# Sharing the normalisation between two engines, and gathering before the stage ends, in a graph attention kernel

## The reference

```python
h = relu(layernorm(x))                       # 12500 x 128
hW = (h @ W_node.T).reshape(N, 4, 32)
e  = (edge_attr @ W_edge.T).reshape(E, 4, 32)
att = sum(concat([hW[src], hW[dst], e]) * a) # per head
att = where(att > 0, att, 0.2 * att)
m = maximum(segment_max(att, dst), 0)
ex = exp(att - m[dst])
denom = segment_sum(ex, dst) + (E - deg) * exp(-m)
out = x + segment_sum(ex / denom[dst] * hW[src], dst)
```

## Time and profile before

| | |
|---|---|
| timed runs, median | 2291.24 us |
| profiled execution, its own time | 2286.65 us |
| its span | 2284.8 us |
| stage 1 / stage 2 / stage 3 | 117.1 / 2129.6 / 38.1 us |
| busy share PE, DVE, ACT, POOL | 53, 70, 26, 73% |
| DMA | 199.98 MB, 87 GB/s |

### The profile page before, as it was taken

The page is one execution under the profiler, slowest core; times in us unless marked ns, Lnnn a source line. Parts: engine busy times, 40 slices in busy tenths (PEclk is TensorE's granted clock), DMA queues, the critical chain, the costliest instruction groups (busy, mean ns, idle before and its releaser), DMA issues. The chain is left out here.

```text
span 2284.8 us, 29035 instructions
## 1 busy us (share of the span) xinstructions
PE 1208.8 (53%) x8459; PEld 1009.0 (44%) x8461; DVE 1597.1 (70%) x4440; ACT 602.1 (26%) x1139; POOL 1676.3 (73%) x1778
## 2 busy tenths in 40 slices
PE   4655555555555555555555554555554554544441
PEld 3514444444444444444444443444444444444441
DVE  7317776767777677776777677676767776777677
ACT  3412222222222222222222222222222222222220
POOL 7877777777777777777777777777777777777740
PEclk8976776777776767776766677777767676666665
DMA  3463233323323233232333333232232322223223
GB/s 120 137 215 98 75 93 80 94 75 86 86 74 98 75 98 75 74 99 74 95 78 84 84 78 94 74 98 74 74 99 75 80 56 56 54 55 86 55 81 145
DMA packets 87796, 199.98 MB, mean 88 GB/s; under 512 B 30142, under 2 KB 49502, under 8 KB 81240
## 3 DMA queue, kind: packets, MB, share of 16 engines
q0 software_dynamic: 53120, 112.30, 21.2%
q1 hardware_dynamic: 32631, 79.28, 10.4%
q10 hardware_dynamic: 1888, 6.56, 0.7%
HBM read 181.70 MB, written 16.31 MB: 87 GB/s over the span
## 5 line engine op out<-in xcount | busy, mean ns | idle before, releaser
L698 POOL DMA_INDIRECT gath<-node_table,src_i x1660 | 1580.5, 952 | 511.5 <-issue 492.4
L778 PE MATMUL bank<-vals,onehot 128*128 128x137 f32 x3328 | 693.1, 386 | 595.2 <-DVE vals L1043 364.9
L778 PEld LDWEIGHTS bank<-vals,onehot 128*128 128x128 f32 x3328 | 643.1, 283 | 620.1 <-DVE vals L1043 375.5
L1077 DVE TENSOR_TENSOR acc<-acc,bank 128x137 f32 x1664 | 495.7, 298 | 426.4 <-PE bank L778 157.3
L853 ACT COPY onehot_t<-ps_oht 128x2048 bf16<-128x2048 bf16 x104 | 194.1, 1866 | 1008.4 <-PE ps_oht L748 984.2
L748 PE MATMUL ps_oht<-ident_b,onehot_b 128*128 128x128 bf16 x1664 | 177.7, 292 | 328.1 <-DVE onehot_b L929 328.1
L862 ACT CAST onehot<-onehot_b 128x384 f32<-128x384 bf16 x624 | 268.7, 474 | 254.3 <-PE bank L778 246.8
L748 PEld LDWEIGHTS ps_oht<-ident_b,onehot_b 128*128 128x128 bf16 x1664 | 161.3, 138 | 336.6 <-DVE onehot_b L929 332.4
L1039 DVE TENSOR_TENSOR vals<-gath,bank 128x2048 f32<-128x2048 f32 x104 | 237.2, 2281 | 1.9 <-ACT bank L866 1.7
L929 DVE TENSOR_TENSOR onehot_b<-bank,rel_s 128x2048 bf16<-128x2048 f32 x104 | 237.1, 2282 | 0.0
L730 PE MATMUL bank<-eattr,w_eatt 128*32 128x512 f32 x392 | 184.5, 615 | 8.0 <-DMA eattr<-edge_attr_in 6.6
(11 more groups left out here) (176 smaller groups left out, 964.9 us busy)
## 6 DMA issues: line engine op xcount, KB each, us to landing
eattr<-edge_attr_in SPq DMA_DIRECT2D x49, 1024.0 KB, 5.7
gath<-node_table,src_i POOLq DMA_INDIRECT x1660
node_table<-onehot_b SPq DMA_DIRECT2D x14, 462.0 KB, 4.0
gath<-x_in SPq DMA_DIRECT2D x14, 448.0 KB, 4.9
gath<-x_in SPq DMA_DIRECT2D x4, 896.0 KB, 5.5
out_dram<-gath ACTq DMA_DIRECT2D x4, 896.0 KB, 3.6
edge_scores<-edge_out SPq DMA_DIRECT2D x49, 64.0 KB, 1.8
edge_s<-edge_scores SPq DMA_DIRECT2D x12, 256.0 KB
```

Source lines behind the costliest of these rows:

```text
L698: nc.gpsimd.indirect_dma_start(out=gath[:, g.r, a * GS + j, :], out_offset=None, in_=table, in_offset=bass.IndirectOffsetOnAxis(ap=src_i[: ...
L778: last = T.matmul(SUM_BANK[b % 3][:, (j % 3) * ACC:(j % 3 + 1) * ACC], onehot[:, b % 3, j % 3, :], vals[:, j, :], start=True, stop=True)
L1077: V.tensor_tensor(a_blk, a_blk, SUM_BANK[(j // 3) % 3][:, (j % 3) * ACC:(j % 3 + 1) * ACC], ALU.add).then_inc(s["added"], 1)
```

## The change

- Each group's normalisation is split: VectorE takes blocks 0 to 2 (`ON_DVE = 3`; all seven of group 0), Pool blocks 3 to 6. `hn` becomes two semaphores.
- Epsilon goes into the square root as its bias, which drops one VectorE instruction. Statistics and reciprocal of g + 3 stand right behind each other on VectorE, and ScalarE's square root of g + 3 (before: g + 2) behind the evacuation of g - 1.
- The slot work moves. Four selection matrices are made in groups 0 to 3 and nine in the last three; the column products and 12 of 13 jobs stand behind the last projection, with the spreads. One source job stays at group 4. The byte casts are in two parts, source early and target at group 11.
- Pool clears in pieces between groups; the tiles' numbers lie in `acc` instead of `eattr`, so that VectorE clears the first 3611 columns at the end. With `eattr` free, SyncE loads the first two edge tiles in the front, and Pool issues the first twelve gathers (`FRONT = 12`) once the table is stored, before the stage ends.
- In the loop's start, the load of the first edge rows comes after the fourth store, and `turn_edges(0)` before edge scores 4 and 5.

```diff
@@ sync
+                    load(0)
                     sp.dma_start(ends_i[:, :, :], tile_ends).then_inc(s_ends, 16)
-                    load(0)
-                    sp.dma_start(tile_rows..., tiles).then_inc(s_tiles, 16)
                     for g in range(1, XBUF):
                         load(g)
+                    sp.dma_start(tile_rows..., tiles).then_inc(s_tiles, 16)
...
+                        if g + XBUF == N_NODE_GROUPS:
+                            for t in range(2):
+                                sp.dma_start(eattr[:, t, :, :]..., ea[t * P:(t + 1) * P, :]).then_inc(s_ea[t], 16)
                         store(g)
@@ gpsimd
-                        for w in range(W):
+                        for w in range(ON_DVE, W):
...
-                    half = (N_BLOCKS + 1) * ACC // 2
-                    pool.memset(acc[:, 0:half], 0.0).then_inc(s_set, 1)
-                    for g in range(N_NODE_GROUPS):
+                    cuts = [in_acc + (acc.shape[1] - in_acc) * n // 5 for n in range(6)]
+                    for g in range(1, N_NODE_GROUPS):
                         normalise(g)
+                        if g >= 2 and small:
+                            t = small.pop()
+                            pool.memset(t.ap(), 1.0 if t is ones else 0.0).then_inc(s_set, 1)
+                        if 3 <= g < 8:
+                            pool.memset(acc[:, cuts[g - 3]:cuts[g - 2]], 0.0).then_inc(s_set, 1)
+                    pool.wait_ge(n_["hn_t_ps"], N_NODE_GROUPS)
+                    for q in range(2):
+                        pool.wait_ge(s_rows[q], 16 * (N_NODE_GROUPS // 2))
+                    pool.wait_ge(s_slots_out, 1)
+                    for j in range(FRONT):
+                        nc.gpsimd.indirect_dma_start(
+                            out=gath[:, 0, j, :], out_offset=None, in_=table, ...).then_inc(s_g[0], 16)
@@ vector
+                    def normalise(g):
+                        dve.wait_ge(n_["rstd"], g + 1)
+                        if g >= 2:
+                            dve.wait_ge(n_["hn_t_ps"], g - 1)
+                        for w in range(ON_DVE if g else W):
+                            last = V.tensor_scalar(hn[g % 2][:, w, :], xg[g % XBUF][:, w, :], ..., ALU.subtract, ALU.mult)
+                        last.then_inc(n_["hn_dve"], 1)
...
+                    at = {0: [0], 1: [1], 2: [2], 3: [3]}
+                    at.update({N_NODE_GROUPS - 3 + n: range(4 + 3 * n, 7 + 3 * n) for n in range(3)})
+                    for g in range(N_NODE_GROUPS):
+                        if g + 2 < N_NODE_GROUPS:
+                            normalise(g + 2)
+                        if g + 3 < N_NODE_GROUPS:
+                            stats(g + 3)
+                            root(g + 3)
+                        for k in at.get(g, ()):
+                            slot_matrix(k)
...
+                    V.memset(acc[:, 0:in_acc], 0.0)
@@ scalar
                     for g in range(N_NODE_GROUPS):
-                        turned(g)
                         if g:
+                            turned(g)
                             evacuate(g - 1)
-                        if g + 2 < N_NODE_GROUPS:
-                            sqrt(g + 2)
-                        for j in JOBS_OF.get(g, ()):
-                            slots_out(j)
...
+                        if g + 3 < N_NODE_GROUPS:
+                            sqrt(g + 3)
+                        if g == SRC_AT:
+                            slots_out(0)
+                        if g == N_NODE_GROUPS - 3:
+                            bytes_of(dst_lo, dst_hi, P + 1)
                     evacuate(N_NODE_GROUPS - 1)
+                    for j in range(1, len(JOBS)):
+                        slots_out(j)
+                        if j >= SPREAD_AT and j - SPREAD_AT < NQ:
+                            block_row_out(j - SPREAD_AT)
@@ the edge loop
-                            for j in range(GS if nxt or a == 0 else LAST):
+                            for j in range(FRONT if g.first and a == 0 else 0, GS if nxt or a == 0 else LAST):
...
-                        load_edge_rows(0)
+                            if t + 1 == CG:
+                                load_edge_rows(0)
...
+                        turn_edges(0, 1)
                         for t in range(AHEAD - 2, AHEAD):
-                            edge_scores(t, 1, 0)
-                        turn_edges(0, 1)
+                            edge_scores(t, 1, 1)
```

More of the change, by code:

```diff
@@ L128, in gat_kernel @@
         vals_flat = vals[:, :, :].rearrange("p s c -> p (s c)")
+        s_ea = [sem(f"eattr_loaded{q}") for q in range(2)]
+        s_g = [sem(f"rows_gathered{q}") for q in range(4)]
+        FRONT = 12
         with ExitStack() as stage:
@@ L331, in _ @@
-                    norm(1)
-                    for k in range(TB):
-                        link(V.tensor_scalar(step1, iota[:, :], before[:, k:k + 1], None, ALU.is_ge))
-                        V.scalar_tensor_tensor(out=sel[:, k, :], in0=iota[:, :], scalar=end[:, k:k + 1],
-                                               in1=step1, op0=ALU.is_lt, op1=ALU.mult).then_inc(s_sel, 1)
-                        dve.wait_ge(s_sel, k + 1)
-                        if k == HALF:
-                            stats(2)
-                        if k == HALF + 3:
-                            norm(2)
@@ L343, in _ @@
+                    keep_tgt(N_NODE_GROUPS - 1)
                     dve.wait_ge(s_cols, 1)
@@ L547, in slots_of @@
                         last.then_inc(s_slots, 1)
+                    pe.wait_ge(s_id, 1)
                     turn(0)
-                    for k in range(HALF + 1):
-                        slot_columns(k)
-                    project(0)
-                    turn(1)
-                    for k in range(HALF + 1, TB):
-                        slot_columns(k)
-                    for g in range(1, N_NODE_GROUPS):
+                    pe.wait_ge(s_w, 48)
+                    pe.wait_ge(s_a, 16 * HEADS)
@@ L567, in _ @@
-                        project(g)
+                        if g == SRC_AT:
+                            slots_of(0)
+                        project(g)
+                    pe.wait_ge(s_tcols, 1)
+                    pe.wait_ge(s_sel, TB)
+                    for k in range(TB):
+                        col = ps_cols[:, NC * k:NC * (k + 1)]
+                        if k:
+                            T.matmul(col, sel[:, k - 1, P:2 * P], tile_cols[:, 1, k - 1, :], start=True, stop=False)
+                        last = T.matmul(col, sel[:, k, 0:P], tile_cols[:, 0, k, :], start=(k == 0), stop=True)
@@ L570, in gat_kernel @@
+                    last.then_inc(s_cols, 1)
+                    for j in range(1, len(JOBS)):
+                        slots_of(j)
+                        if j >= SPREAD_AT and j - SPREAD_AT < NQ:
+                            spread(j - SPREAD_AT)
+                    pe.wait_ge(s_slots_out, len(JOBS))
+                    pe.wait_ge(s_brow, NQ)
+                    T.matmul(b5[:, 0:NG], ones_b[0:1, :], rel_s[0:1, 0:NS:G], start=True, stop=True).then_inc(s_first, 1)
         OW = 2 * NODE_GROUP
```

192 lines of the change are left out of this document (90 added, 102 removed).

## The result

| | before | after |
|---|---|---|
| median of 4 timed runs each, one chip | 2290.75 us | 2266.49 us |
| ratio, 95% interval | | 0.9885 [0.9874, 0.9897] |
| profiled execution, its own time | 2286.65 us | 2261.55 us |
| its span | 2284.8 us | 2259.7 us |
| stage 2's first PE instruction | 117.1 us | 108.3 us |

24.3 us faster by the medians, 25.1 by the profiled executions, 24.1 of them by the start of the stream. The forecast of the median was 2267, the measured one is 2266.49.

The account below looks back on a forecast made before the run. Pool's unbroken stream of gathers was taken as the bound. Starting in effect at 94.4 instead of 117.9, 23.5 us earlier, it gives 2263.2; with 4.6 for the median 2267.7, taken as 2267, range 2255 to 2278.

Parts of the forecast that it names:

- What bounds it: Edge loop: Pool's 1660 back-to-back gathers, 1.257 us each, are the clock; a microsecond earlier start saves a microsecond.
- Part 1, the pace: Front's groups: the load of x queued behind a store sets 4.9 us a group, where Pool's 5.6 did before.
- Part 2, the ends: Front's start and end: twelve gathers from 90.9 to 106, stage 2 from 108.7, Pool resuming at 109.5.
- E(0): Front: time at which the rows of group 0 are out, forecast 25.7 us.
- E(13): Front: time at which the rows of group 13, the last, are out, forecast 86.6 us.
- 17.6 behind the last projection, 1.5 for the end, 2 for the clock: Front's end: slot work, leaving the stage and a slow TensorE clock add 21.1 us to 87.6, so stage 2 begins at 108.7.
- Part 3, the edge loop: Edge loop: twelve gathers fewer save 15.1 us, stream 23.5 earlier; VectorE's first additions have room of 7 or stall Pool 1.
- A: Rival, front: lockstep, each VectorE tile waits out a Pool tile, 5.9 us a group; 2277; 12 in 100.
- B: Rival, front: the load of x is no limit, 4.2 us a group, 7 us less, 2260; 20 in 100.
- C: Rival, edge loop: late flags starve the stream at gather 72, costing 2 to 5 us, 2269 to 2272; 12 in 100.
- D: Rival, front: the hold between VectorE and Pool makes it slower than before, 2297 to 2310; 3 in 100.
- E: Rival, front's end: the twelve gathers wait for the last store or source slots and end after the stage; 2269; 3 in 100.

Follow-up runs that it names:

- the loads ahead: Changed kernel, but SyncE issues the load of x for group g+5 ahead of the store of group g, not behind it; 2260.34 us, ratio 0.9878.
- the one-tile run: Changed kernel, but VectorE normalises one tile of seven instead of three, Pool six; on the second chip, 3355.71 us, ratio 0.994.
- the late clearing: Changed kernel, but Pool's five pieces of clearing stand behind its last normalisation tile instead of between the groups; 2271.28 us, ratio 0.9927.

## Why the prediction was right

**What bounds it: right.** The stream begins 24.1 earlier and the span is 25.1 shorter. The rest is 0.6 over 1660 gathers and 0.4 behind them. Of the edit's parts, the twelve gathers (10.2 of the stream's start) and the three tiles (against one, 10.9 of the first gather's start, on the second chip) were tried by themselves. What the moved slot work and the new order at the loop's start are worth was not.

**Part 1, the pace: right in size, by the loop it named for half of the groups.** Forecast 4.9, measured 4.90. From 46 us on, loads behind stores set it (the loads ahead removed all waits for x). In the clearing groups Pool's own work did, 5.0 to 5.3 without a pause: it stayed so with the loads ahead, grew to 6.6 with six tiles, and without the pieces the load took over at 4.83. The prediction had this term at 5.1, above its own 4.9, and still said that none of the three engines was the slowest loop. That 4.9 came out even so is luck: the two limits are of nearly one size (the first five intervals of stores average 4.96, the last five 4.84). Three tiles cost 1.0, not 0.75.

**Part 2, the ends: right in the sum, wrong in one step.** E(0) 25.7 (forecast 25.7), E(10) 74.8 (75.3), E(13) 85.8 (86.6), gathers from 91.0 to 105.9 (90.9 to 106). Then the step "17.6 behind the last projection, 1.5 for the end, 2 for the clock" failed: selection matrices ended at 85.3 instead of 87.6, the tail took 16.7, the clock was 1.00 from 85 to 100, and the slot work was done at 102.0 instead of 107.2. In its place Pool's twelve gathers ended the stage, 105.9, and leaving it took 2.4: 108.3, where 108.7 was forecast. Two errors of 5 us cancelled, by luck. The words "its twelve being just done" had the two side by side; the larger of the two should have been taken with its own price for the end.

**Part 3, the edge loop: right.** Into stage 2: turned scores used at 34.4 (35), flags in at 50.8 (46 to 54), first additions done at 71.9 (69 to 77). Pool wanted them at 184.3 and had them at 180.2. VectorE's clearing took 3.07 (3.1).

**Rivals.** A fell with the one-tile run and the 1.0 for three of L310. B (no load limit, 4.2 a group) was wrong as a description of after; with the loads ahead, groups without clearing take 3.49, those with it Pool's 5.0 to 5.3. C came to a wait of VectorE's of 12.8 and none of Pool's. D's hold is real, as the late clearing shows, but the pieces between the groups made VectorE's 0.30 into 0.88 and no group over 5.6. Of E the condition came true, not the price: the twelve waited for the last store and ended the stage, 3.9 after VectorE.

**The prediction's reading of the earlier trace rows was wrong in one place.** The 8.94 us for seven of Pool's tiles did not lie beside the L333 rows of 0.43; beside those (18.7 to 25.6 us) a tile took 0.99 to 1.00. Five of the seven took 0.79 to 0.92, and two stood for nearly the whole of a two-source instruction of VectorE's:

```profile
32.73 1.93 DVE L342 TENSOR_TENSOR onehot<-eattr 128x1664 bf16<-128x1664 int32 x1
...
35.74 1.89 DVE L348 TENSOR_TENSOR onehot_t<-ident_b,t 128x1664 bf16<-128x1664 bf16 x1
...
L240 POOL TENSOR_SCALAR gath<-gath,mv,st x2: 923/1709/2495, 31.8 to 32.7; 128x128 f32<-128x128 f32 x2
L240 POOL TENSOR_SCALAR gath<-gath,mv,st x2: 790/1554/2317, 35.2 to 36.0; 128x128 f32<-128x128 f32 x2
```

So the hold goes both ways, and what the prediction called partial was two nearly full holds of a Pool tile: 2.50 and 2.32 instead of 0.79. In after these two instructions (77.87 and 87.25) have none of Pool's tiles beside them.

## What to carry to other kernels

When one engine's unbroken stream sets the time, price an edit by how much earlier the stream is under way, and count work that this engine does ahead of a stage's end as holding that end for all. Before moving a long clearing on GpSimd, look which VectorE instruction stands beside it and who waits behind that one: 8.5 us in an idle stretch of Pool put the table's last rows 7.9 later. And where a sum gives two limits of nearly one size, say which groups have which. Look also at what stands ahead of a store in its queue when its buffer is needed again.

## What the runs showed that was not expected

- **The same kernels take 1.47 times as long on two other chips.** Two stretches of equal length, the front up to 90 us and 78 us of the edge loop, after on the first chip, then on the second (busy us of PE, PEld, DVE, ACT, POOL, then clock, DMA share, GB/s):

```profile
0.00:90.00 90.00, 53.52 (x388) 48.68 (x389) 68.56 (x335) 42.18 (x104) 53.07 (x74) 0.91 0.62 190
108.00:186.00 78.00, 47.95 (x278) 23.17 (x279) 34.02 (x76) 19.43 (x29) 58.54 (x62) 0.78 0.52 157
```

```profile
0.00:90.00 90.00, 54.39 (x387) 49.76 (x387) 67.70 (x330) 41.76 (x104) 53.25 (x74) 0.91 0.63 190
112.00:190.00 78.00, 25.46 (x103) 8.39 (x101) 8.72 (x10) 4.95 (x7) 49.15 (x52) 0.63 0.37 106
```

  The front is the same. The stalls begin with the gathers: ScalarE then stands for something that the profile calls remote (1229.1 us before one line on the third chip; the first shows no such wait), and VectorE and PE wait for it. Gathers are as long as before, 954 and 952 ns. What it is stays open; the change is worth 27 to 28 us there by the medians (3375.18 to 3347.14, 3371.11 to 3344.0), about as on the first chip.

```profile
ACT onehot_t L882 <- remote: 1229.1, 43, 35.5
```

- **Leaving a stage behind gathers costs 2.3 to 2.5 us**, in the run without them 0.3 (105.65 after 103.34 with nine gathers, 105.66 after 103.19 with the loads ahead; 103.27 after 102.94 with none). In after VectorE and TensorE stood idle meanwhile; what the time goes into stays open.
- **A VectorE memset runs at 0.84 ns a column** (8.35 for 9952) beside gathers and slows none of them, while Pool's own clears shut VectorE's casts out.
